# Bidirectional scan stage: the sums of numerator and denominator moved from Vector to TensorE

## What is computed

```python
decay = exp(-exp(w)) * (0.5 + 0.5 * tf)          # per channel and sequence
ek, ekv = exp(minimum(k, 30)), exp(minimum(k, 30)) * v      # here k = v = f
nf, df = forward scans:  a = a * decay + ekv ;  b = b * decay + ek
nb, db = the same scans from the last step to the first
euk = exp(minimum(u + k, 30))
num = nf + nb - ekv + euk * v
den = df + db - ek + euk
out = sigmoid(r) * (num / maximum(den, 1e-8)) * (0.8 + 0.2 * tf)    # here r = x
```

## Time and profile before

| | before |
|---|---|
| median of 3 runs | 1300.31 us |
| lowest, highest | 1295.31, 1301.39 us |
| profiled execution | 1298.61 us |
| its span in the profile | 1296.8 us |
| mean granted TensorE clock | 0.949 of full speed |

### The profile page before, as it was taken

The page is one execution under the profiler, slowest core; times in us unless marked ns, Lnnn a source line. Parts: engine busy times, 40 slices in busy tenths (PEclk is TensorE's granted clock), DMA queues, the critical chain, the costliest instruction groups (busy, mean ns, idle before and its releaser), DMA issues. The chain is left out here.

```text
span 1296.8 us, 16339 instructions
## 1 busy us (share of the span) xinstructions
PE 1129.0 (87%) x4986; PEld 604.1 (47%) x4986; DVE 809.0 (62%) x1215; ACT 561.3 (43%) x1501; POOL 342.2 (26%) x348
## 2 busy tenths in 40 slices
PE   0289997899968999999978997987997879979998
PEld 0045553455534444444436773446853348644443
DVE  7799995999956676667664443696504974224222
ACT  4355664556542232323232454675724757410110
POOL 0336654266550000000010000575502755200000
PEclk9989999899987999999987999898998979979999
DMA  7000000000033000000130001200000000000000
GB/s 282 24 1 1 1 1 1 1 0 1 21 147 141 1 1 0 1 0 0 36 162 1 2 2 43 113 1 1 2 1 1 0 0 0 0 9 1 1 0 32
DMA packets 5491, 33.38 MB, mean 26 GB/s; under 512 B 528, under 2 KB 1936, under 8 KB 3536
## 3 DMA queue, kind: packets, MB, share of 16 engines
q1 hardware_dynamic: 5424, 32.61, 6.5%
HBM read 31.56 MB, written 1.05 MB: 25 GB/s over the span
## 5 line engine op out<-in xcount | busy, mean ns | idle before, releaser
L815 POOL TENSOR_TENSOR decays<-decays,scores 128x768 f32<-128x768 f32 x64 | 119.8, 1874 | 135.3 <-ACT decays L750 135.1
L1103 PE MATMUL ph<-h,weights 128*128 x256 | 116.9, 601 | 0.0
L583 PE MATMUL pg<-h,weights 128*128 (+1 forms) x136 | 67.0, 616 | 55.8 <-PEq L361 54.3
L2149 POOL TENSOR_TENSOR spare<-m,weights 128x256 f32<-128x256 f32 x80 | 91.1, 1158 | 91.5 <-DVE m L2170 90.5
L750 ACT ACTIVATE decays<-pcum,neg_cum 128x256 f32<-128x256 f32 (+1 forms) x256 | 86.2, 425 | 7.1 <-PE pcum L636 6.8
L883 DVE SCALAR_TENSOR_TENSOR conv<-px,pp,conv 128x510 f32<-128x510 f32 (+2 forms) x102 | 75.9, 744 | 16.0 <-ACT conv L722 13.6
L583 PE MATMUL px<-h,weights 128*128 x136 | 72.5, 658 | 13.0 <-DVE conv L883 13.0
L1160 ACT ACTIVATE up<-ph 128x512 f32<-128x512 f32 x44 | 26.3, 597 | 129.6 <-PE ph L1103 129.6
L1103 PEld LDWEIGHTS ph<-h,weights 128*128 128x128 f32 x256 | 49.4, 193 | 62.2 <-issue 62.2
L1407 POOL TENSOR_TENSOR prob_gqa<-prob_gqa,inverse_gqa 128x128 f32<-128x128 f32 (+1 forms) x128 | 62.0, 506 | 59.4 <-DVE inverse_gqa L1397 57.8
L1767 POOL MEMSET halves<- 64x64 f32 x4 | 0.6, 145 | 279.4 <-POOLq L1011 279.2
(11 more groups left out here) (350 smaller groups left out, 2588.1 us busy)
## 6 DMA issues: line engine op xcount, KB each, us to landing
weights<-in_w_mixer SPq DMA_DIRECT2D x2, 2048.0 KB, 18.6
weights<-in_w_moe SPq DMA_DIRECT2D x2, 1536.0 KB, 8.3
moe_rest<-in_w_moe SPq DMA_DIRECT2D x2, 1536.0 KB, 13.5
weights<-in_w_gqa SPq DMA_DIRECT2D x1, 3072.0 KB, 10.3
weights<-in_w_gqa SPq DMA_DIRECT2D x1, 2048.0 KB, 14.8
weights<-in_w_moe SPq DMA_DIRECT2D x1, 1920.0 KB, 8.7
weights<-in_w_mixer SPq DMA_DIRECT2D x1, 1536.0 KB, 12.4
weights<-in_w_moe SPq DMA_DIRECT2D x1, 1152.0 KB, 12.6
```

The lines of the kernel that those rows point to most:

```text
L583: op = nc.tensor.matmul(out[0:m, :], w[:, col + k * m:col + (k + 1) * m], net.h[:, ds(i * PAIR + k * TOK, TOK)], start=(k == 0), stop=(k = ...
L815: nc.gpsimd.tensor_tensor(decays[:, head % 4], decays[:, head % 4], scores[:], ALU.mult).then_inc(decay_scaled, 1)
L1103: op = nc.tensor.matmul(out[:], wt[:, n * D + k * P:n * D + (k + 1) * P], net.h[:, ds(i * PAIR + k * TOK, TOK)], start=(k == 0), stop=(k = ...
L2149: op = nc.gpsimd.tensor_tensor(out[:, :, s, :], src[:, :, 1 - s, :], sin[:, None, s, :].to_broadcast([P, 4, HALF]), ALU.mult)
```

## The change

In the first stage the Vector engine no longer subtracts e and adds the parts. TensorE multiplies each of eight terms per pair by an identity matrix (or by minus the identity) and accumulates them in PSUM, one bank per sum, sequence and pair (8 banks). Vector keeps add_u, e times f, E times f (E is euk), the four scan groups, the maximum and the factor; the last two now read PSUM, and the inverse is worked in place in m. Scalar no longer copies e. `CondUnit` loses the variant that only this stage used. GpSimd makes the minus-identity once ident and cb are loaded; these two loads move ahead of x. Vector's order of steps is new, and the factor and h of pair 0 stand after the first two steps of pair 1.

```diff
-    def scalar_invert(self, turn):
...
-        if self.bounded is not None:
-            stages = [
-                add_u, scan(net.den, net.e, den_done),
-                scan(net.den_b, net.e_pair, den_b_done, True), own,
-                combine(net.den, net.den_b, den_done, den_b_done),
-                combine(net.den, net.euk, den_done, own_done), bound,
-                e_times_f, scan(net.num, net.ev_pair, num_done),
-                scan(net.num_b, net.ev_pair, num_b_done, True), own_times_f,
-                combine(net.num, net.num_b, num_done, num_b_done),
-                combine(net.num, net.ev_pair, num_done, ev_done),
-            ]
...
+    MINUS_E, MINUS_EV, DEN_FORWARD, EUK, DEN_BACK, EUV, NUM_FORWARD, NUM_BACK = range(1, 9)
+    def of_batch(x, b):
+        return x.rearrange("p (k b t) -> p k b t", k=KT, b=BB)[:, :, b, 1:SEG]
...
+        minus = mem.enter_context(nc.sbuf_tensor("minus_ident", [P, P], F32))
+        sums = [[[mem.enter_context(nc.psum_tensor(f"{n}_sum{pair}{b}", [P, KT, SEQ], F32))
+                  for b in range(BB)] for n in ("den", "num")] for pair in range(PAIRS)]
...
+            sp.dma_start(net.ident[:], dram["ident"]).then_inc(net.consts_loaded, 16)
+            sp.dma_start(net.cb[:], dram["cb"][:, 0:CB_SEL]).then_inc(net.consts_loaded, 16)
             sp.dma_start(net.x[:], dram["x"]).then_inc(net.x_loaded, 16)
-            sp.dma_start(net.cb[:], dram["cb"][:, 0:CB_SEL]).then_inc(net.consts_loaded, 16)
-            sp.dma_start(net.ident[:], dram["ident"]).then_inc(net.consts_loaded, 16)
...
+            pool.wait_ge(net.consts_loaded, 32)
+            nc.gpsimd.tensor_scalar(minus[:], net.ident[:], -1.0, None, ALU.mult) \
+                .then_inc(minus_ready, 1)
...
+            def add_term(pair, which, lhs, x, start, stop):
+                for b in range(BB):
+                    op = nc.tensor.matmul(sums[pair][which][b][:], lhs[:], of_batch(x, b),
+                                          start=start, stop=stop)
+                op.then_inc(term_added, 1)
+
+            for pair in range(PAIRS):
+                pe.wait_ge(e_padded, PAIRS)
+                add_term(pair, 0, minus, net.e[:, unit_cols(pair)], True, False)
+                pe.wait_ge(ev_made, (pair + 1) * KT)
+                add_term(pair, 1, minus, net.ev_pair[:], True, False)
+                pe.wait_ge(den_scanned, pair * 2 * KT + KT)
+                add_term(pair, 0, plus, net.den[:], False, False)
+                pe.wait_ge(euk_ready, pair + 1)
+                add_term(pair, 0, plus, net.euk, False, False)
+                pe.wait_ge(den_scanned, (pair + 1) * 2 * KT)
+                add_term(pair, 0, plus, net.den_b[:], False, True)
+                pe.wait_ge(euv_made, (pair + 1) * KT)
+                add_term(pair, 1, plus, euv, False, False)
+                pe.wait_ge(num_scanned, pair * 2 * KT + KT)
+                add_term(pair, 1, plus, net.num[:], False, False)
+                pe.wait_ge(num_scanned, (pair + 1) * 2 * KT)
+                add_term(pair, 1, plus, net.num_b[:], False, True)
...
+            spread_decay(0)
+            exp_u(0)
             tanh_h()
             nc.scalar.preload_act_table_set("natural_log_exp_and_others")
+            invert(0)
+            spread_decay(1)
+            exp_u(1)
+            invert(1)
...
+            def bound(pair):
+                dve.wait_ge(*added(pair, DEN_BACK))
+                for b in range(BB):
+                    v.tensor_scalar(of_m(pair, b), sums[pair][0][b][:], 1e-8, None, ALU.max) \
+                        .then_inc(bounded, 1)
+            def factor(pair):
+                dve.wait_ge(inverted, 2 * (pair + 1))
+                dve.wait_ge(*added(pair, NUM_BACK))
...
             for pair in range(PAIRS):
+                add_u(pair)
+                e_times_f(pair)
+                if pair:
+                    factor(pair - 1)
+                    make_h(pair - 1)
+                for k in range(KT):
+                    scan(pair, k, net.den, net.e, den_scanned, DEN_FORWARD, False)
+                for k in range(KT):
+                    scan(pair, k, net.den_b, net.e, den_scanned, DEN_BACK, True)
+                euk_times_f(pair)
+                scan(pair, 0, net.num, net.ev_pair, num_scanned, NUM_FORWARD, False)
+                scan(pair, 1, net.num, net.ev_pair, num_scanned, NUM_FORWARD, False)
+                bound(pair)
+                for k in range(KT):
+                    scan(pair, k, net.num_b, net.ev_pair, num_scanned, NUM_BACK, True)
+            factor(PAIRS - 1)
+            make_h(PAIRS - 1)
```

More of the change, by code:

```diff
@@ L281, in bound @@
             v.wait_ge(*den_done[k])
[L282 to L286, removed]
+            den_done[k] = link.mark(v.tensor_scalar(net.den[:, here], net.den[:, here], 1e-8,
+                                                    None, ALU.max))
         def invert(part):
@@ L297, in factor @@
             v.wait_ge(*num_done[KT - 1])
-            if self.inverted is not None:
-                v.wait_ge(self.inverted, 2 * (turn + 1))
             shape = dict(k=KT, b=BB)
@@ L414, in _ @@
             v = nc.vector
-            link = Links(dve, links)
             dve.wait_ge(net.params_loaded, 16)
@@ L442, in _, with columns, add_u @@
             dve.wait_ge(e_padded, PAIRS)
-            for pair in range(PAIRS):
-                for step in unit.vector(link, pair, pair):
-                    step()
-                make_h(pair)
+            def columns(pair, k):
+                n = BB * SEG
+                return slice(k * n, (k + 1) * n), slice(pair * UNIT + k * n,
+                                                        pair * UNIT + (k + 1) * n)
+            def add_u(pair):
+                if pair:
+                    dve.wait_ge(*added(pair - 1, EUK))
+                    dve.wait_ge(euv_made, pair * KT)
+                for k in range(KT):
+                    here, both = columns(pair, k)
+                    op = v.tensor_scalar(net.euk[:, here], net.f[:, both],
+                                         net.pp[:, PP_U + k:PP_U + k + 1], 30.0, ALU.add, ALU.min)
+                op.then_inc(u_ready, 1)
@@ new lines, in e_times_f, with scan @@
+            def e_times_f(pair):
+                if pair:
+                    dve.wait_ge(*added(pair - 1, MINUS_EV))
+                    dve.wait_ge(num_scanned, pair * 2 * KT)
+                for k in range(KT):
+                    here, both = columns(pair, k)
+                    v.tensor_tensor(net.ev_pair[:, here], net.e[:, both], net.f[:, both],
+                                    ALU.mult).then_inc(ev_made, 1)
+            def scan(pair, k, out, x, done, term, reverse):
+                here, both = columns(pair, k)
+                if pair:
+                    dve.wait_ge(*added(pair - 1, term))
+                dve.wait_ge(decay_spread, KT * BB * pair + (k + 1) * BB)
+                if x is net.ev_pair:
+                    dve.wait_ge(ev_made, pair * KT + k + 1)
+                order = slice(None, None, -1) if reverse else slice(None)
+                data = x[:, both if x is net.e else here]
+                v.tensor_tensor_scan(out[:, here][:, order], net.decay[:, here][:, order],
+                                     data[:, order], 0.0, ALU.mult, ALU.add).then_inc(done, 1)
@@ new lines, in euk_times_f, with of_m @@
+            def euk_times_f(pair):
+                if pair:
+                    dve.wait_ge(*added(pair - 1, EUV))
+                dve.wait_ge(euk_ready, pair + 1)
+                for k in range(KT):
+                    here, both = columns(pair, k)
+                    v.tensor_tensor(euv[:, here], net.euk[:, here], net.f[:, both], ALU.mult) \
+                        .then_inc(euv_made, 1)
+            def of_m(pair, b):
+                return net.m[:, pair * PAIR:(pair + 1) * PAIR].rearrange(
+                    "p (k b t) -> p k b t", k=KT, b=BB)[:, :, b, :]
@@ new lines, in bound @@
+            def bound(pair):
+                dve.wait_ge(*added(pair, DEN_BACK))
+                for b in range(BB):
+                    v.tensor_scalar(of_m(pair, b), sums[pair][0][b][:], 1e-8, None, ALU.max) \
[3 more added lines that the diff above has]
+                dve.wait_ge(*added(pair, NUM_BACK))
+                for b in range(BB):
+                    op = v.scalar_tensor_tensor(of_m(pair, b), sums[pair][1][b][:],
+                                                net.scol[:, pair * BB + b:pair * BB + b + 1],
+                                                of_m(pair, b), ALU.mult, ALU.mult)
+                op.then_inc(factor_made, 1)
+                dve.wait_ge(factor_made, pair + 1)
```

72 lines of the change are left out of this document (46 added, 26 removed).

## The result

The changed kernel's median over four executions is 1281.55 us (1278.40 to 1287.03), that of the kernel before beside it on the same chip 1297.81 (1293.99 to 1301.39): 16.3 us less, a ratio of 0.9874 with a 95% interval of 0.9834 to 0.9915. The forecast was 8.0 us less, 1292.3 in a range of 1287.5 to 1299. The profiled execution took 1278.4 us, with a span of 1276.6 and a granted clock of 0.958 (before: 1298.61, 1296.8, 0.949).

What follows compares the result with a forecast made beforehand. The first stage was taken to be bound by Vector's queue; 12.0 + 0.2 - 1.4 - 1.0 - 1.8 = 8.0 us, taken off the median 1300.3, gave 1292.3 us, range 1287.5 to 1299.

Steps and rivals of the forecast that it cites:

- Vector's loss of 12.0 us: First stage: E minus e and the additions leave Vector, 6.0 us per pair, 12.0 us in all.
- The stage as a whole: First stage, Vector's queue from 10.0 to 53.6 us: 8.0 us shorter after all gains and losses.
- The maximum from PSUM: First stage, Vector: reading PSUM takes nearer 0.69 us than 0.67 us for two halves, 1.4 us more in all.
- The term of 1.72 us: First stage, TensorE: each of 16 terms takes 1.72 us at 2.4 GHz or 3.42 us at 1.2 GHz.
- The first maximum's wait: First stage, pair 0: Vector's maximum waits about 1.0 us for TensorE, ends 0.3 and 2.0.
- The last factor's wait: First stage, pair 1: the exposed last numerator term and its hand-over cost 1.8 us ahead of the factor.
- The mixer's first matmul: Start of the mixer: at 46.3 us instead of 54.33, by the ends 45.6 to 47.3.
- (a): First stage: ident lands late or the clock falls in pair 1's pause; both leave about 5 us, 1295.3; chance 0.20.
- (c): First stage: TensorE never leaves 1.2 GHz and becomes the bound, 13.8 us more, 1314.1; chance 0.07.
- a microsecond taken out of it is a microsecond of the whole: First stage: as one engine's queue, its saving passes fully to the total, provided nothing else ends later.
- Rival (b): Mixer: starts 8 us earlier, but its own chain eats the gain, 1299 to 1300; chance 0.08.
- the door: Start of the mixer, TensorE's clock after idling: taken as zero, between 1.7 us gained and 1.3 us lost.

Runs made afterwards that it cites:

- run 3: Kernel before without E minus e and the four groups of additions in the first stage, so its output is not the sum; 1284.19 us, ratio 0.9859.
- 11: Kernel before with three throwaway matmuls in latent attention, without E minus e and the four groups of additions; 1275.14 us, ratio 0.9811.
- run 1: The changed kernel again, no edit, five rounds beside the kernel before; 1281.13 us, ratio 0.9863.
- run 6: Changed kernel with 20 one-column memsets on Vector while it waits for parameters; 1289.84 us, ratio 0.9919.
- run 5: Changed kernel with its first stage delayed by four long products on Vector; 1300.11 us, ratio 0.9995.
- run 8: Changed kernel with three throwaway matmuls in TensorE's waits at latent attention's first turned maximum; 1277.21 us, ratio 0.9825.
- run 9: Changed kernel with three throwaway matmuls in latent attention and 20 one-column memsets on Vector; 1281.99 us, ratio 0.9865.
- run 2: Kernel before with 44 matmuls on TensorE in the first stage whose result nobody reads; 1298.71 us, ratio 0.9974.

## Why the prediction was wrong in size

**What held.** Vector's loss of 12.0 us (12.3 alone in runs 3 and 11). The stage as a whole, 8.3 us shorter in the first profile and 7.3 in run 1, against 8.0. The maximum from PSUM, 679 ns in the groups by form against 690. GpSimd's negation, 0.53 us and done at 9.2, as forecast; TensorE's start, 10.09 against 10.0. The term of 1.72 us, with the moving operand in two runs of 256 columns. The first maximum's wait: 0.58 us, 1.68 in run 1, 1.90 in run 6, against 1.0 with ends of 0.3 and 2.0. The last factor's wait, 2.16 against 1.8. In pair 1 the clock held through a pause of 1.66. The mixer's first matmul, 45.97 and 47.45 in two profiles, against 46.3 with ends of 45.6 and 47.3. Rivals (a) and (c) did not come: ident was there in time, and the clock rose 3.3 to 6.0 us after TensorE's start in the profiles of this kernel and its variants. Two small slips of the working change nothing: (a) leaves 8.0 - 1.6 - 2.1 = 4.3 us, not 5, and the low end adds up to 1287.9, not 1287.5. After the first four instructions the terms stay at 1.72 us from start to start, with the banks changing at each, so the rule of the Trainium skill cited under (c) did not bite.

**What failed.** The step "a microsecond taken out of it is a microsecond of the whole, provided nothing else ends later". Rival (b) looked at the mixer alone and asked what ties it to an absolute time, not about the stages behind it. The forecast added up the stage alone, 8.0 us, and asked only what could be lost downstream. It took each later stage to cost what it did in that one profile; but two of them held costs that depend on things other than their own work, and the door, which it set at zero, did not always stay there:

- *Latent attention at half clock*, 8.9 us in the profile and the largest part of the miss. It stood in that profile as 10.0 of 10 us busy at 0.50, and the clock row of its page, in slices of 32.4 us, is at 8 and 7 from 648 to 713 us (slices 21 and 22) where most others have 9:

```profile
PEclk9989999899987999999987999898998979979999
```

  Six of the eight unfilled profiles have it. That the kernel before runs into it in most executions and the changed one in few is inferred from the spread of times and mean clocks.
- *Vector's stall at pair 2*, 2.05 us. By the runs, it comes and goes with the packets of instructions, 40 or 41 in the eight profiles with a stall and 35 in the six without, and it follows the length of Vector's code (runs 3 and 6). In each of the eight, Vector has no record for 2.8 to 3.8 us behind the jump back of the loop, and one instruction packet (two in run 5) starts in the idle stretch. In the six, its next record comes within 0.3 us of the jump, and after the packet that all fourteen have about the jump the next comes 13 us later. That it is a load of Vector's code rests on this; the packet's row does not name the engine that it serves. The Trainium skill, "Advanced Engine Details and Errata" (ISA Cache), gives a cache line of 256 instructions and two such lines; by that a stream 20 instructions shorter can need one line less. The packets counted here are of 8 KB each and fall by five, so the count alone does not say which of them is such a line.
- *The door*, the term set to zero between +1.7 and -1.3. It drew 1.5 in the first profile and 0.2 in run 1. Of the eight profiles of the changed kernel and its variants, two (the first and run 8) had it warm.

Added to the 8.4 us by which the mixer began earlier: 8.9 + 2.05 + 1.5, less 0.7 of drift, makes the 20.2 between the two profiles. In the medians, with the stretch present in part of the executions of each, it is 16.3, and 19.5 in run 1.

**What stays open.** Why the changed kernel mostly escapes the low stretch. Less code on Vector does not do it alone (run 3's profile has it), an early mixer does not (run 6 has it), and run 1 has one execution in six that looks like it by time and clock. The traces show one regularity: in the six unfilled profiles with the stretch the clock first fell 0.2 to 1.5 us after the first turned maximum, where TensorE has just idled for 2 us; in the two without, it fell 5.2 us after it and was up again 3.4 us later. What decides where the fall lands no run shows. What is shown is what the stretch costs and that three matmuls prevent it. Whether the padding itself makes late starts and cold doors likelier (run 9) stays open too, and so do the 2.4 to 2.9 us behind grouped attention.

## What to carry to other kernels

Compare two profiles landmark by landmark before explaining a difference: here more than half of it lay 170 to 730 us behind the last changed line. Ask of the profile before not only what could be late next, but which later stretches are dearer than their work (TensorE fully busy at half clock, an idle engine whose named releaser had long ended), since any change may flip them either way. And where executions scatter by 12 us, fill the stretch that scatters first, and measure the change after that.

## What the runs showed of the hardware

- The granted clock stayed at 0.50 for 20.5 us while TensorE was busy for all of it (kernel before, from 699.1), and in run 2 for 27.3 us with 26.3 busy. Of the 175 matmul records of the 20.5 us, 120 are f32 on 32 rows. The same rounds ran at 1.00 throughout in the filled kernels, so the work alone does not set the level. Three f32 matmuls of 128 rows ahead of it, in waits of 2.0 and 1.0 us, kept it at 1.00 until the end of the rounds in all six filled profiles. The Trainium skill, "TensorE: Matmul & The Clock Gate" (HAM oscillation), ties a low clock to idle gaps. Such gaps (2.0 and 1.0 us) do stand ahead of the stretch, but from 700 to 710 us there is no idle time at all and the clock does not come back, so for that the measurement decides.
- After a pause of 3.5 to 3.6 us ahead of the mixer the clock was still up in one execution of the changed kernel (pg 1.90 us after 3.57) and down in another (3.23 after 3.54).
- Twenty instructions fewer on one engine removed 2.4 us of idle time at the jump back of its loop, 170 us further on; sixteen fewer (and a stage 8 us later) did not, and left 3.74.
